# The running sum of a selective scan: VectorE adds terms in pairs, GpSimd adds the pair sums

## What is computed

```python
A_bar = exp(d_c[..., None] * A)
BX = d_c[..., None] * B_c[:, :, None, :] * x_c[..., None]
A_cum = exp(minimum(cumsum(log(maximum(A_bar, EPS)), axis=1), LOG_CLAMP))
wcum = cumsum(BX / maximum(A_cum_sh, EPS), axis=1)
h_chunk = A_cum * wcum / maximum(A_bar, EPS) + h[:, None] * A_cum
y_c = einsum('bls,blds->bld', C_c, h_chunk) + D_param * x_c
```

## Time and profile before

| | |
|---|---|
| three runs, median (lowest to highest) | 6189.16 us (6188.1 to 6192.53) |
| span of the profiled execution | 6189.9 us |
| TensorE busy (matmuls) | 5686.4 us, 92% |
| VectorE busy | 5633.4 us, 91% |
| ScalarE busy | 3734.6 us, 60% |
| GpSimd busy | 2744.1 us, 44% |

### The profile page before, as it was taken

The page is one execution under the profiler, slowest core; times in us unless marked ns, Lnnn a source line. Parts: engine busy times, 40 slices in busy tenths (PEclk is TensorE's granted clock), DMA queues, the critical chain, the costliest instruction groups (busy, mean ns, idle before and its releaser), DMA issues.

```text
span 6189.9 us, 77161 instructions
## 1 busy us (share of the span) xinstructions
PE 5686.4 (92%) x16152; PEld 2632.6 (43%) x16152; DVE 5633.4 (91%) x7057; ACT 3734.6 (60%) x4618; POOL 2744.1 (44%) x2138
## 2 busy tenths in 40 slices
PE   5999999999999999999999999999999999999997
PEld 2444444444444444444444444444444444444443
DVE  4999999999999999999999999999999999999997
ACT  3666665665666666656666666566566666665664
POOL 2444444444444444444444444444444444444443
PEclk9999999999999999999999999999999999999998
DMA  1121121121111211211212112112121121121120
GB/s 64 11 17 19 14 17 15 14 19 13 16 18 14 17 16 14 19 15 14 19 13 17 16 14 19 15 14 19 13 16 18 14 17 15 14 19 15 14 17 11
DMA packets 157893, 104.23 MB, mean 17 GB/s; under 512 B 121008, under 2 KB 121008, under 8 KB 157488
## 3 DMA queue, kind: packets, MB, share of 16 engines
q1 hardware_dynamic: 157488, 100.71, 17.8%
HBM read 42.63 MB, written 16.78 MB: 10 GB/s over the span
## 4 chain that ended last, share of the span: by engine, by line
PE 37%; DVE 31%; issue 20%; ACT 3%; DVEq 2%; ACTq 0%; DMA 0%; SPq 0%
PE state L971 13%; DVE acc L1321 11%; PE cum L961 10%; DVE term L1311 6%; PE fbank L866 5%; DVE conv L1167 4%; DVE conv L1159 2%; PE ebank L936 2%; PE ebank L916 2%; PE fbank L879 2%; DVE xn L1277 1%; ACT xiT L568 1%; DVE dx L1222 1%; DVE delta L1213 1%; PE fbank L850 1%
## 5 line engine op out<-in xcount | busy, mean ns | idle before, releaser
L699 ACT ACTIVATE decay<-cum,neg_a 128x1024 f32<-128x1024 f32 x1024 | 1138.6, 1112 | 1944.8 <-PE cum L961 1942.4
L971 PE MATMUL state<-sources,tri_upto 128*128 128x512 f32 x4096 | 1980.6, 606 | 187.4 <-DVE term L1311 187.1
L473 POOL TENSOR_SCALAR room<-total,limit 128x1024 f32<-128x1024 f32 x1024 | 1352.8, 1321 | 1653.9 <-ACT cum L704 1448.2
L463 POOL TENSOR_SCALAR step<-delta,limit 128x1024 f32<-128x1024 f32 x1024 | 1243.4, 1214 | 1661.2 <-PE cum L961 1038.5
L961 PE MATMUL cum<-step,tri_before 128*128 128x512 f32 x4096 | 1940.7, 596 | 3.5 <-DVE sources L1298 3.5
L1311 DVE SCALAR_TENSOR_TENSOR term<-state,crow,decay 128x1024 f32<-128x1024 f32 x1024 | 1308.8, 1278 | 247.4 <-PE state L971 135.9
L1321 DVE TENSOR_TENSOR acc<-acc,term 128x1024 f32<-128x1024 f32 x1024 | 1459.2, 1425 | 0.2
L1298 DVE SCALAR_TENSOR_TENSOR sources<-cum,brow,dx 128x1024 f32<-128x1024 f32 x1024 | 1303.1, 1273 | 12.1 <-ACT cum L704 12.1
L971 PEld LDWEIGHTS state<-sources,tri_upto 128*128 128x128 f32 x4096 | 744.5, 191 | 1068.5 <-issue 941.7
L961 PEld LDWEIGHTS cum<-step,tri_before 128*128 128x128 f32 x4096 | 777.7, 192 | 941.7 <-issue 935.6
L704 ACT ACTIVATE cum<-room,pos_a 128x1024 f32<-128x1024 f32 x1024 | 1143.6, 1117 | 17.6 <-POOL room L473 2.7
(11 more groups left out here) (125 smaller groups left out, 3972.7 us busy)
## 6 DMA issues: line engine op xcount, KB each, us to landing
hfirst<-hrows SPq DMA_DIRECT2D x496, 64.0 KB, 3.9
xt<-in_x SPq DMA_DIRECT2D x64, 256.0 KB, 2.6
hrows<-term SPq DMA_DIRECT2D x1024, 4.0 KB, 1.7
xres<-in_x SPq DMA_DIRECT2D x64, 256.0 KB, 2.7
out_x<-xres SPq DMA_DIRECT2D x64, 256.0 KB, 2.1
gate_last<-gate SPq DMA_DIRECT2D x512, 0.5 KB, 2.1
win<-in_w_in SPq DMA_DIRECT2D x2, 2048.0 KB, 10.7
hrows<-hrows SPq DMA_DIRECT2D x64, 64.0 KB, 2.3
```

Of the source, the lines that this page charges most:

```text
L463: nc.gpsimd.tensor_scalar(step[s % 2][:, :], delta[t.parity][:, :], limit[:, s:s + 1], 0.0, ALU.min, ALU.max).then_inc(step_ready, 1)
L473: nc.gpsimd.tensor_scalar(room[:, :], total[:, :], limit[:, s:s + 1], 0.0, ALU.min, ALU.max).then_inc(room_ready, 1)
L699: nc.scalar.activation(decay[s % 4][:, :], cum[s % 2][:, :], ACT.Exp, scale=neg_a[:, s:s + 1]).then_inc(decay_ready, 1)
L971: last = nc.tensor.matmul(state[:, cols], tri_upto[:, :], source[s % 2][:, cols], start=True, stop=True)
```

## The change

VectorE no longer adds each term to acc. In every even slot it adds the even term before the last to the odd one that it has just made (`pair`), in place in the even term's buffer, and GpSimd adds this sum to acc (`add_pair`), at the end of its own pass of the same slot. Odd terms have a buffer of their own; even terms alternate between the two others. The pair waits until SP's DMA has saved the last row of the even term. A term in an odd slot waits for the pair before, a term in an even slot for GpSimd's add of two pairs before. The third term buffer takes the space of xn2, which now lies in the tile of xn, with two new waits for it on VectorE. The last pair of a tile is handled in slot 0 of the next. `end_gate` and the carry path wait for the last pair's add.

```diff
+def pair_at(tile, slot):
+    return tile.n * (NS // 2) + slot // 2 + 1
+def term_at(slot):
+    return 2 if slot % 2 else slot // 2 % 2
...
-        term = [sb(f"term{i}", [P, DI]) for i in range(2)]
+        term = [sb(f"term{i}", [P, DI]) for i in range(3)]
...
-        xn2 = sb("xn2", [P, D])[:, :]
+        xn2 = xn[:, :]
...
-                sp.dma_start(hmain[t.parity][s:s + 1, :], term[s % 2][P - 1:P, :]).then_inc(last_saved[s % 2], 16)
+                sp.dma_start(hmain[t.parity][s:s + 1, :], term[term_at(s)][P - 1:P, :]).then_inc(last_saved[s % 2], 16)
...
+            def add_pair(t, s):
+                pool.wait_ge(paired, pair_at(t, s))
+                if s == 1:
+                    pool.wait_ge(front_pool, at(FRONT_POOL, t, "skip"))
+                else:
+                    pool.wait_ge(added, pair_at(t, s - 2))
+                stand(pool)
+                sums = acc[t.parity][:, :]
+                nc.gpsimd.tensor_tensor(sums, sums, term[term_at(s - 1)][:, :], ALU.add).then_inc(added, 1)
...
                     if s == 0 and prev is not None:
+                        add_pair(prev, NS - 1)
                         finish(prev)
+                    if s > 0 and s % 2 == 0:
+                        add_pair(t, s - 1)
                     if more:
                         if s == 14:
                             skip(nxt)
...
                 if prev is not None:
                     dve.wait_ge(norm_pe, at(NORM_PE, prev, "xnT"))
+                if t.shift(-4) is not None:
+                    dve.wait_ge(end_act, at(END_ACT, t.shift(-4), "q"))
...
-            def end_scale(t):
+            def end_scale(t, in_xn):
                 prev = t.shift(-1)
                 if prev is not None:
                     dve.wait_ge(end_act, at(END_ACT, prev, "q"))
+                if in_xn is not None:
+                    dve.wait_ge(norm_pe, at(NORM_PE, in_xn, "xnT"))
...
             def term_of(t, s):
-                user, old = before(t, s, 2)
-                if user is not None:
-                    dve.wait_ge(added, slot_at(user, old))
-                    dve.wait_ge(last_saved[s % 2], ring_at(user, old))
+                if s % 2:
+                    user, old = before(t, s, 2)
+                    if user is not None:
+                        dve.wait_ge(paired, pair_at(user, old))
+                        dve.wait_ge(last_saved[1], ring_at(user, old))
+                else:
+                    user, old = before(t, s, 4)
+                    if user is not None:
+                        dve.wait_ge(added, pair_at(user, old))
...
-            def add(t, s):
-                sums = acc[t.parity][:, :]
-                if s == 0:
-                    dve.wait_ge(front_pool, at(FRONT_POOL, t, "skip"))
-                else:
-                    dve.wait_ge(added, slot_at(t, s - 1))
+            def pair(t, s):
+                dve.wait_ge(last_saved[0], ring_at(t, s - 1))
                 dve.wait_ge(term_ready, slot_at(t, s))
-                nc.vector.tensor_tensor(sums, sums, term[s % 2][:, :], ALU.add).then_inc(added, 1)
+                sums = term[term_at(s - 1)][:, :]
+                nc.vector.tensor_tensor(sums, sums, term[term_at(s)][:, :], ALU.add).then_inc(paired, 1)
...
-                    if s > 0:
-                        add(t, s - 1)
-                    elif prev is not None:
-                        add(prev, NS - 1)
+                    if s == 0 and prev is not None:
+                        pair(prev, NS - 1)
+                    elif s > 0 and s % 2 == 0:
+                        pair(t, s - 1)
```

More of the change, by code:

```diff
@@ L241, in mamba_block @@
         term_ready = sem("term_ready")
+        paired = sem("paired")
         added = sem("added")
@@ L486, in finish @@
                     pool.wait_ge(carry_cleared, t.n + 1)
-                    pool.wait_ge(added, slot_at(t, NS - 1))
+                    pool.wait_ge(added, pair_at(t, NS - 1))
                     for s in range(1, NS):
@@ L531, in body, with end @@
                             skip(nxt)
-            whole(pool, start, body, finish)
+            def end(t):
+                add_pair(t, NS - 1)
+                finish(t)
+            whole(pool, start, body, end)
         @block.scalar
@@ L1232, in end_gate @@
             def end_gate(t):
-                dve.wait_ge(added, slot_at(t, NS - 1))
+                dve.wait_ge(added, pair_at(t, NS - 1))
                 dve.wait_ge(carry_added, carry_at(t))
@@ L1310, in term_of @@
                     done(nc.vector.tensor_tensor(state[:, :], state[:, :], abar, ALU.add), state_full, t.n + 1)
-                nc.vector.scalar_tensor_tensor(out=term[s % 2][:, :], in0=state[:, :], scalar=crow[t.parity][:, s:s + 1],
+                nc.vector.scalar_tensor_tensor(out=term[term_at(s)][:, :], in0=state[:, :], scalar=crow[t.parity][:, s:s + 1],
                                                in1=decay[s % 4][:, :], op0=ALU.mult, op1=ALU.mult).then_inc(term_ready, 1)
-            def add(t, s):
-                sums = acc[t.parity][:, :]
-                if s == 0:
-                    dve.wait_ge(front_pool, at(FRONT_POOL, t, "skip"))
-                else:
-                    dve.wait_ge(added, slot_at(t, s - 1))
+            def pair(t, s):
+                dve.wait_ge(last_saved[0], ring_at(t, s - 1))
                 dve.wait_ge(term_ready, slot_at(t, s))
-                nc.vector.tensor_tensor(sums, sums, term[s % 2][:, :], ALU.add).then_inc(added, 1)
+                sums = term[term_at(s - 1)][:, :]
+                nc.vector.tensor_tensor(sums, sums, term[term_at(s)][:, :], ALU.add).then_inc(paired, 1)
             def finish(t):
@@ L1419, in body @@
                         if s == 15:
-                            end_scale(prev)
+                            end_scale(prev, t.shift(2) if more2 else None)
             def end(t):
                 term_of(t, NS - 1)
-                add(t, NS - 1)
+                pair(t, NS - 1)
                 finish(t)
@@ L1433, in end @@
                 end_refine(t)
-                end_scale(t)
+                end_scale(t, None)
                 end_out(t)
```

## The result

Four runs of the changed kernel took 6539.39 us in the median (6535.53 to 6547.01), the kernel before beside them 6188.65: a ratio of 1.0565, with an interval of 1.055 to 1.058. The change costs 351 us, where 49 were forecast. The sign is right; the size lies far outside the range.

The account below looks back on a forecast made before the run. TensorE (92% busy) and VectorE (91%) were taken to bound the kernel together. 34 tiles at +1.4 us, 29 at 0 and +1.2 gave +49 on 6189.9: 6239, or 6238 as median; range 6080 to 6306.

Parts of the forecast that it names:

- Slots 12 and 13, the main cost: GpSimd's add, held by delta, delays step 0 and room 15; growth 15, total0's copy and total1 are 2.5 us late.
- Slots 5 to 8: Slots 5, 7 lose a VectorE add; slot 6's ygT fix waits for GpSimd's add, +1.5 us; lateness ends at 1.4.
- The taps: Slot 6: VectorE's taps are charged nothing; the other end is one GpSimd instruction, 1.1 us more a tile.
- Rival C: GpSimd's queue becomes the bound in slots 6 to 9, 2.2 us a tile, 141 us: 6330; chance 0.09.
- What costs nothing: New pair wait, third buffer, xn2 in xn and the carry path, said not to be run, are charged nothing.
- I take 0 for such a tile: Slots 14 to 0: behind a hardware-loop jump TensorE waited 2.40 us anyway, so the lateness vanishes: 0 us.
- Rival A, VectorE's relief: TensorE's waits for VectorE go, as 730 us leave that engine: 5987 at best, 6088 more likely; chance 0.35.
- The sum by its own terms: Of 64 tiles, 34 at +1.4 us, 29 behind a jump at 0, and +1.2 at the program's end: +49 us.

Follow-up runs that it names:

- m12: Changed kernel with only the GpSimd add of pair (10, 11) moved from the end of its slot 12 to the end of slot 13: 6344.53 us.
- m6: Changed kernel with only the GpSimd add of pair (4, 5) moved from the end of its slot 6 to the end of slot 7: 6357.29 us.
- c0: Changed kernel with the last pair's GpSimd add in slot 0 moved behind the signal carry_merged: 6490.93 us.
- alias: Kernel before with only xn2 put in the tile of xn, with its two new waits on VectorE: 6190.12 us.
- noadd: Changed kernel with each GpSimd add replaced by a clear of 8 columns of acc, so the sum over states is left out: 5997.45 us.
- The three edits together: Changed kernel with adds of pairs (4, 5) and (10, 11) one slot later and the last pair's add behind carry_merged: 6214.05 us.
- mall_c0: Changed kernel with GpSimd's adds of all pairs 0 to 11 one pass later and the last pair's add behind carry_merged: 6208.09 us.
- v1: `mall_c0` with the GpSimd add of pair (12, 13) moved from slot 14 to the end of slot 15 as well: 6190.0 us.
- memset: Changed kernel with three clears of acc that read nothing in place of each GpSimd add, sum over states left out: 6421.7 us.

## Why the prediction was right and wrong

**Slots 12 and 13, the main cost: right.** The chain ran as written, 2.3 us more of waiting against 2.5, and undoing it alone (`m12`) takes the wait back to 19.8 us in all. What the step left out is what 195 us for a wait of 145 shows: the clock that falls behind the wait, in 57 of 63 tiles, and ScalarE's small steps behind the late copies.

**"Slots 5 to 8" and "The taps": wrong in direction and size; this is the step that failed.** It let the add start "just ahead of" the fix and charged VectorE 1.5 us. The fix went first and the taps kept GpSimd out, so the price fell on GpSimd's queue: 4.32 + 3.28 us for add and step. The taps were charged nothing, though the earlier trace rows had a step held for 1 us by them: an add that starts together with a row of taps has the whole row in front of it. `m6` puts this place at 182 us of the 351. By the forecast the tile's lateness shrinks here, from 2.0 to 1.4 us; measured, the place adds 182/64 = 2.8 us to it. Rival C named the queue of slots 6 to 9 and priced it at 2.2 us a tile, close to the 2.24 us that TensorE waits; but it was given 0.09 and stood alone, where in fact it came on top of slot 13 and with the clock behind it. TensorE's wait is for the step, at the head of C's chain; that the room, growth and silu block behind it cost time as well isn't shown.

**"What costs nothing": wrong for the carry path.** "Its lines have no instructions in the trace" is true of the branch that adds carries. The other branch has a signal, raised by the sequencer, for which ScalarE waits: 48 us (`c0`). A timeline leaves it out, but the trace of the kernel before has it, once a tile, when asked for that line by itself:

```profile
L505 POOLq EVENT_SEMAPHORE  x64: 17/17/17, 199.4 to 6138.5; - x64
```

The rest of that step held: `alias` shows the shared tile to be free.

**"I take 0 for such a tile": wrong.** The two waits come 64 and 62 times, at 2.6 and 2.2 us in the mean, so tiles behind a jump pay too.

**Rival A, VectorE's relief:** true of VectorE and not of the time. `noadd` gives 5997 us, and the term wait fell to 62.3 us. But the relief isn't all kept: VectorE is busy 5273.6 us in the changed kernel and 4941.8 in `noadd` with the same instructions, so GpSimd's adds shut it out for 332 us, 45% of the 730 us taken from it. Against the kernel before, the taps of slot 5 (L1190), xres (L1323) and xn (L1175) rose by 108, 108 and 100 us.

The sum by its own terms: forecast +49. The three edits together give back 325 of 351 us, and the rest goes with `mall_c0` and `v1`, at 6190. The 102 us of added busy time are about what the granted clock took (108 us); the forecast had no term for it.

A page of the Trainium skill was weighed on the way. "SBUF — State Buffer" (Who interferes with whom) says that the lock is held for a whole instruction and that issue order decides who blocks. The 4.32 us row agrees with the second part; by the first, a waiting add should have come in after the first tap of about 0.3 us, and it waited for eight. The step of 3.28 us begins at 3055.09, 0.12 us ahead of its row of taps, and is held for that whole row too, as in some 60 other tiles; if its start can be read that finely, the order of issue doesn't explain it. The forecast had put that rule down as worth some 60 us more; here the trace went the other way. The same section says that a GpSimd instruction which only writes doesn't contend with a two-input one of VectorE's; the clear beside the taps in `memset` agrees.

## What to carry to other kernels

Work moved to a less busy engine is paid for by what stands behind it in that engine's queue, signals that a timeline doesn't show included: list the waiters of every later instruction and signal, and put the new work behind the ones that TensorE or ScalarE need next (here 71 us instead of 424). Then look for the rows of two-input VectorE instructions beside each place; where one can't be avoided, leave that piece on VectorE. Two waits in one tile can cost more than their sum, as the clock may fall, so gains from removing them one at a time don't add up.

## What the runs showed of the hardware that was not expected

- VectorE instructions with two SBUF inputs that follow each other closely hold out a waiting GpSimd instruction for the whole row: eight taps of 2.17 us in all made an add 4.32 us and a step 3.28, though the step's row begins 0.12 us before the taps'. A waiter gets in only sometimes (the taps of slot 5, 643 ns against 440).
- The granted clock fell behind waits of TensorE of 2.59 us (to 0.65 over the next 3 us) and of 2.24 us (0.62). It did so behind the wait of slot 13 in 57 of 63 tiles when the tile had another wait of 2.24 us some 40 us earlier, and in 18 of 63 when it had not.
- A semaphore that a sequencer raises by itself waits for the instructions queued ahead of it: with an add of 3.20 us in front, ScalarE waited 243.2 us in all for it.
